# Level 1 of a fused two-layer convolution kernel: the attention chain moved ahead of the large filter, one feature half moved to another PSUM bank

## The reference, cut to what matters

```python
for i in range(LEVELS):
    y = x                                   # for i > 0: mean over blocks of 2**i x 2**i
    y = relu(conv(y, ds_w3[i], ds_b3[i], pad=d, dil=d))
    feats.append(conv1x1(y, ds_w1[i], ds_b1[i]))
def conv_att2(x, ...):                      # for each level's features
    f_att, f_idt = x[:, :16], x[:, 16:]
    pooled = f_att.mean(axis=(2, 3))
    hdn = gelu(pooled @ kg_w1.T + kg_b1, approximate=False)
    ker = (hdn @ kg_w2.T + kg_b2)           # a 3 x 3 filter for each image and channel
    out = concat([conv(f_att, lk_filter, pad=6) + depthwise(f_att, ker), f_idt])
    return conv1x1(out, fus_w, fus_b)
```

## Time and profile before

| | us |
|---|---|
| median of 3 runs | 2907.32 (2903.90 to 2908.01) |
| the profiled execution | 2903.58 |
| its span, first to last instruction | 2901.8 |
| TensorE busy | 2649.9 (91%) |
| VectorE busy | 2140.3 (74%) |
| level 1 | 58 to 655 of the span |

### The profile page before, as it was taken

The page is one execution under the profiler, slowest core; times in us unless marked ns, Lnnn a source line. Parts: engine busy times, 40 slices in busy tenths (PEclk is TensorE's granted clock), DMA queues, the critical chain, the costliest instruction groups (busy, mean ns, idle before and its releaser), DMA issues. The chain is left out here.

```text
span 2901.8 us, 38918 instructions
## 1 busy us (share of the span) xinstructions
PE 2649.9 (91%) x12262; PEld 2127.6 (73%) x12262; DVE 2140.3 (74%) x2968; ACT 1054.7 (36%) x1641; POOL 627.5 (22%) x663
## 2 busy tenths in 40 slices
PE   5899999987999699999999698999966999999998
PEld 4677777766888588888887577777755777777776
DVE  5444444454454688888888889999877999999998
ACT  1211111111100588999898322222203333233232
POOL 6544443403220444444443100000001000000000
PEclk9999999997988799999999799999977999999999
DMA  7222222201000777777776223333443333333342
GB/s 148 62 74 70 68 71 71 64 17 37 13 13 8 161 220 218 219 219 215 216 215 173 95 103 149 148 134 134 153 172 111 94 106 108 92 116 99 94 122 58
DMA packets 288702, 338.04 MB, mean 116 GB/s; under 512 B 24816, under 2 KB 243824, under 8 KB 274288
## 3 DMA queue, kind: packets, MB, share of 16 engines
q1 hardware_dynamic: 280736, 334.74, 39.2%
q10 hardware_dynamic: 7888, 2.29, 0.5%
HBM read 211.60 MB, written 122.62 MB: 115 GB/s over the span
## 5 line engine op out<-in xcount | busy, mean ns | idle before, releaser
L168 PE MATMUL ps_all<-vh,u_h 128*128 128x512 f32 x960 | 385.0, 401 | 28.3 <-DVE vl L2818 27.4
L170 PE MATMUL ps_all<-vh,u_l 128*128 128x512 f32 x960 | 383.6, 400 | 0.0
L169 PE MATMUL ps_all<-vl,u_h 128*128 128x512 f32 x960 | 383.1, 399 | 0.0
L2727 ACT ACTIVATE vh<-rt,gn 128x528 fp32r<-128x528 f32 x192 | 130.4, 727 | 446.1 <-DVE rt L2795 314.6
L168 PE MATMUL ps_all<-vh,t_h 128*128 128x512 f32 x576 | 231.2, 401 | 23.7 <-DVE vl L1873 23.7
L168 PEld LDWEIGHTS ps_all<-vh,u_h 128*128 128x128 f32 x960 | 181.0, 189 | 81.9 <-issue 35.4
L169 PE MATMUL ps_all<-vl,t_h 128*128 128x512 f32 x576 | 230.0, 399 | 0.0
L170 PE MATMUL ps_all<-vh,t_l 128*128 128x512 f32 x576 | 229.2, 398 | 0.0
L170 PEld LDWEIGHTS ps_all<-vh,u_l 128*128 128x128 f32 x960 | 181.1, 189 | 46.3
L169 PEld LDWEIGHTS ps_all<-vl,u_h 128*128 128x128 f32 x960 | 181.3, 189 | 45.5
L1712 POOL TENSOR_TENSOR zr<-zr,z 128x256 f32<-128x256 f32 x128 | 122.5, 977 | 342.8 <-DMA xr<-in_x 342.8
(11 more groups left out here) (401 smaller groups left out, 6733.5 us busy)
## 6 DMA issues: line engine op xcount, KB each, us to landing
xr<-in_x SPq DMA_DIRECT2D x128, 256.0 KB, 3.6
x_layer<-xr SPq DMA_DIRECT2D x64, 512.0 KB, 2.7
xq<-x_layer SPq DMA_DIRECT2D x32, 1024.0 KB, 4.9
x_layer<-xq SPq DMA_DIRECT2D x32, 1024.0 KB, 3.8
out<-ot SPq DMA_DIRECT2D x64, 512.0 KB, 5.2
xw<-in_x SPq DMA_DIRECT2D x112, 288.0 KB, 4.3
xc<-in_x SPq DMA_DIRECT2D x120, 256.0 KB, 3.9
xw<-x_layer SPq DMA_DIRECT2D x16, 1152.0 KB, 8.7
```

The lines of the kernel that those rows point to most:

```text
L168: pe.matmul(o, wh, xh, start=first, stop=False, skip_group_check=True)
L169: pe.matmul(o, wh, xl, start=False, stop=False, skip_group_check=True)
L170: return pe.matmul(o, wl, xh, start=False, stop=last, skip_group_check=True)
L2727: act.activation(vh[:, v % 2, n, :, :].rearrange("p a b -> p (a b)"), rt[:, n, :, :].rearrange("p a b -> p (a b)"), ACT.Identity, scale=gn ...
```

## The change

It does five things in the bodies of level 1:

- Half 1 of the features goes to `ps_stat`. With that TensorE waits for two copies out of `ps_q`, not for three.
- TensorE does `chain_hidden` behind the third of the eight feature pixels and `chain_taps` behind the last, ahead of its wait for the remainders. Both leave the filter.
- ScalarE does the Gelu ahead of the four roundings.
- ScalarE counts `f_h` up after each piece, and VectorE waits for each piece.
- VectorE does `chain_pooled_dve` ahead of the remainders, and `chain_taps_dve` right behind them, ahead of the statistics or the preparation of layer 1.

```diff
+            feat = (ps_q[:, 1, :], ps_stat)
...
+                        chain_act(act, i, 1, chain, hdn_s)
                         for hf in range(2):
                             act.wait_ge(qful, Q * i + QF + hf + 1)
                             p0 = 3 + NB1 * hf
-                            ps = ps_q[:, 1 - hf, 0:NB1 * (NQ1 + 2)].rearrange("p (n q) -> p n q", q=NQ1 + 2)
+                            ps = feat[hf][:, 0:NB1 * (NQ1 + 2)].rearrange("p (n q) -> p n q", q=NQ1 + 2)
                             for hp, c0 in inner:
-                                ins = act.activation(fh[hp, p0:p0 + NB1, c0:c0 + NQ1], ps[hp, :, c0 - 1:c0 - 1 + NQ1],
-                                                     ACT.Identity, bias=b1a[hp, 1:2])
-                            ins.then_inc(f_h, 1)
-                        chain_act(act, i, 1, chain, hdn_s)
+                                act.activation(fh[hp, p0:p0 + NB1, c0:c0 + NQ1], ps[hp, :, c0 - 1:c0 - 1 + NQ1],
+                                               ACT.Identity, bias=b1a[hp, 1:2]).then_inc(f_h, 1)
...
                         for k in range(3):
                             plain(i, k)
+                        chain_pooled_dve(dve, i, ((1, 1),), pooled_s, chain)
                         for hf in range(2):
-                            dve.wait_ge(f_h, 2 * i + hf + 1)
                             p0 = 3 + NB1 * hf
-                            ps = ps_q[:, 1 - hf, 0:NB1 * (NQ1 + 2)].rearrange("p (n q) -> p n q", q=NQ1 + 2)
-                            for hp, c0 in inner:
+                            ps = feat[hf][:, 0:NB1 * (NQ1 + 2)].rearrange("p (n q) -> p n q", q=NQ1 + 2)
+                            for k, (hp, c0) in enumerate(inner):
+                                dve.wait_ge(f_h, 4 * i + 2 * hf + k + 1)
                                 ins = dve.scalar_tensor_tensor(fl[hp, p0:p0 + NB1, c0:c0 + NQ1],
...
                             ins.then_inc(qfree, 1)
-                        chain_pooled_dve(dve, i, ((1, 1),), pooled_s, chain)
+                        chain_taps_dve(dve, i, 1, chain, ker_s)
                         if not last:
                             for c in range(NX - 3, NX):
                                 prep_chunk(i + 1, c)
                         if last:
                             conv5_shift(1, 1)
                             conv5_shift(1, 2)
-                        chain_taps_dve(dve, i, 1, chain, ker_s)
...
-                        pe.wait_ge(qfree, Q * i + QF + 2)
+                        pe.wait_ge(qfree, 2 + Q * i + 2)
                         for j, (dr, dc) in enumerate(PIX):
...
-                                mm = product(pe, ps_q[:, 1 - hf, 0:NB1 * (NQ1 + 2)].rearrange("p (n q) -> p n q", q=NQ1 + 2),
+                                mm = product(pe, feat[hf][:, 0:NB1 * (NQ1 + 2)].rearrange("p (n q) -> p n q", q=NQ1 + 2),
                                              fa_h[w], fa_l[w], rh[v], rl[v], j == 0, j == 7)
                                 if j == 7:
                                     mm.then_inc(qful, 1)
+                            if j == 2:
+                                chain_hidden(pe, i, 1, 1, pooled_s, chain)
+                        chain_taps(pe, i, 1, hdn_s, chain)
                         pe.wait_ge(qfree, 2 + Q * i + QL)
...
-                        between = {4: lambda: chain_hidden(pe, i, 1, 1, pooled_s, chain),
-                                   10: lambda: chain_taps(pe, i, 1, hdn_s, chain),
-                                   NSTAT: lambda: dyn.at(pe, i, DSTEPS)}
+                        between = {NSTAT: lambda: dyn.at(pe, i, DSTEPS)}
```

## The result

The changed kernel takes 2883.7 us in the median of 4 runs (2880.7 to 2885.1), the kernel before 2907.6; the ratio is 0.9921, interval 0.9909 to 0.9933. The forecast was 2880, a ratio of 0.9906. The profiled execution took 2880.7 us with a span of 2878.9.

What follows compares the result with a forecast made beforehand. TensorE, busy 2649.9 of 2901.8 us, was taken as the bound. -0.65 - 0.04 - 2.25 - 0.49 = -3.43 us an image, x8 = -27.4, gave 2876.2 profiled, 2880 median; own range 2875 to 2886, whole range 2868 to 2891.

Steps and rivals of the forecast that it cites:

- the likeliest case: Whole kernel: the parts' gains add up at an unchanged clock, 2880 us, own range 2875 to 2886, chance 0.64.
- Part 1: Start of level 1's features: half 1 in `ps_stat`, no wait for the third `z` copy, -0.65 us an image.
- Part 2: Hidden matmul from filter to behind the third feature pixel: filter 0.28 shorter, features 0.24 longer, together -0.04 us.
- Part 3: Taps from the filter into the pause, under cover of the rounding: -2.25 us an image, free at 2.4 GHz.
- Part 4: End of the pause: VectorE starts behind one rounding piece, so the filter starts 0.49 us earlier an image.
- the loss that its bounds allowed for: Remainder pieces in the pause: up to 1.5 us lost if sharing a bank doubled VectorE's piece length.
- rival B: Pause: taps fall into the slow clock and outlast the roundings by 1.1 us; 2892 us, chance 0.13.
- Rival A: Pause and filter: the filled pause keeps the clock up, 12 us more gained, 2868 us, chance 0.15.
- Rivals C and D: C: feature halves no longer run side by side, 2930, chance 0.03. D: another level 1 chain takes over, 2904, chance 0.05.
- -3.43 us an image at an unchanged clock ... I take 0: Level 1: the parts' gains summed per image, with the clock's effect, bounded by +1.5 and -1.5, taken as 0.

Runs made afterwards that it cites:

- x11_again: The changed kernel run once more, nothing altered, for a second profile: 2879.5 us, ratio 0.9908 to the kernel before.
- x4_taps_back: The changed kernel with the taps back in the filter ahead of tile 10, as one block: 2906.5 us.
- x9_before_fill: The kernel before with ten extra 128 x 512 matmuls, result unread, in its pause: 2903.1 us.
- x1_bank: The kernel before with only half 1 of the features in the other bank and a wait for two copies: 2907.5 us.
- x2_pieces: The kernel before with only a semaphore step for each rounding piece, VectorE waiting for each: 2905.0 us.
- x3_chain: The kernel before with only hidden matmul, taps, Gelu and VectorE's chain steps moved; still three copies and whole halves waited for: 2890.9 us.
- x7_split: x4_taps_back with three taps each ahead of tiles 6, 10 and 14 instead of nine ahead of tile 10: 2905.4 us.

## Why the prediction was right, and where it was not

The time, the direction and the likeliest case held. The sum of the terms over eight images, as cut from the two profiles, against the forecast: waits ahead of the features -4.8 (forecast -5.2); features +2.6 (+1.9); the pause -2.3 (-3.9); the filter -21.1 (-20.2); together -25.6 (-27.4). The span shortened by 22.9; the 2.7 between are lost behind level 1, and their cause stays open (x11_again).

- **Part 1** gave its 0.6 in "rest". The third copy was late for nobody.
- **Part 2**: 0.30 an image for 0.24. The nearest row had features of 48 columns, these have 288.
- **Part 3** is right in size: the filter lost 2.6 to 2.7 (2.53 with the hidden matmul), and the taps start 0.37 behind the last pair for 0.21. What the forecast did not see is that moving the taps also takes away the exposure to a second slow stretch (six of eight images in x4_taps_back).
- **Part 4** is right at its place (0.51 behind `fh`, pause 3.05 in four images), and the loss that its bounds allowed for did not come: VectorE's four pieces took 2.02 us, two of them while ScalarE read the other half of the same bank. The Trainium skill (PSUM — Partial Sum Buffer, PSUM bank collisions) says that engines in different quadrants of one bank do not collide, and the trace agrees. In the other four images the taps reach into the slow clock and outlast the roundings, with pauses of 3.22 to 3.65 (3.26 to 3.74 in five images of x11_again). That is rival B in half of the images and at about a third of its 1.1 us: 0.40 us each, 0.29 on the mean of images 2 to 6.
- **Rival A** did not come: 74 slow filter matmuls for 74. The granted clock falls in the pause (five images) or behind it (three), though the third image's pause has TensorE busy for 3.20 of 3.20 us. The Trainium skill (TensorE: Matmul & The Clock Gate, What's actually happening) has the clock follow how busy TensorE recently was; taken at its word, as the rival took it, the trace does not agree. In x4_taps_back and x9_before_fill the taps are themselves what the clock falls behind. **Rivals C and D** fell: the pairs stay pairs, and no new wait of TensorE arose.
- **The step that failed** is "-3.43 us an image at an unchanged clock ... I take 0", in so far as the terms were added as if each stood alone. x1_bank and x2_pieces gained 0 and 1.5 us for their forecast 5.2 and 3.9, x3_chain 15.5, together 17; all in one gained 24 to 26. So it is in part luck that the plain sum came near: two of its terms were worth next to nothing alone, and the taps were worth more than their term beside them (23 us between x4_taps_back and the changed kernel, for 16 expected). The clock's share is no constant beside the terms: six kernels with the taps in the filter, whose features, pause and rest together differ by up to 1.0 us an image, all have images of 74.75 to 74.98 us. In x1_bank, x2_pieces and x4_taps_back the filter takes the difference back with more slow matmuls, those behind the taps among them; in x9_before_fill such a stretch eats most of what the filled pause won. In x7_split two more seams take most of it.

## What to carry to other kernels

A block of tiny matmuls inside a run of full ones can cost more than its own length: here TensorE's clock fell behind it in none to seven of eight images, by kernel, and the clock took back small gains elsewhere. Take such a block out, into a pause that something else makes anyway, before polishing waits, and test the parts together too, since each alone can measure as nothing. Before moving work into a pause, ask what it covers where it stands: the fourth 1x1 covered a wait of the same length.

## What the runs showed of the hardware that I had not expected

- ScalarE and VectorE read the two partition halves of one PSUM bank at the same time at full speed: VectorE's four pieces take 2.02 us for 2.00 in separate banks (two of the four coincide with a read of the same bank).
- Filling the pause of the kernel before kept the clock at 1.00 there and made it fall behind the taps instead, 11 to 12 us after the filter's start, in seven of eight images where none had it. The time fell by 3.8 us where ten slow matmuls an image had been priced at 12.
- The feature pairs (64 x 288) start 0.26 us apart at either level: 178 steps at 1.2 GHz and 166 at 2.4 GHz in the kernel before have the same mean. So a slow stretch costs nothing there, and when it moves from the features into the filter, it begins to cost.
- 18 passes on 8 rows take 2.16 us at 2.4 GHz and 3.08 where the granted clock of the stretch is 0.70, though they move one column each.
